# Cross-attention and sine feed-forward in one launch: the order of the first group

## The chip, the core and the metric

One core of a Trainium2 chip runs one program. The metric is the device time of a run in microseconds. The median of three runs of the kernel before is 244.93 us (244.87 to 245.15).

## The reference

The input x has 2 batches of 2048 rows of 512; the context has 2 batches of 77 keys of 512, with a mask of keys.

```
Q = layernorm(x) @ Wq + bq;  K = ctx @ Wk + bk;  V = ctx @ Wv + bv
scores = Q K^T / sqrt(512), masked keys at -1e9
x2 = x + softmax(scores) V @ Wo + bo
h = layernorm(x2)
out = x2 + sqrt((h @ cos(theta + theta_noise))^2 + (h @ sin(phi + phi_noise))^2)
```

## The kernel before

The rows go in 8 groups of 512, that is 4 tiles of 128 rows; groups alternate between the two batches. In a group n, TensorE multiplies the transposed h of each tile (`hT`, made by a DMA transpose from `h_split`) by the cosine matrix (real part, `re_bank`) and the sine matrix (imaginary part, `im_bank`). Values and weights are split into high and low fp16 halves, so each product is three matmuls per chunk of 128 (L503 to L505), 12 for a tile and part. Between them stand the attention matmuls of group n + 1 (`attend`) and the score matmuls of group n + 2.

All engines' queues are written out by hand, as lists of calls. Semaphores hold the order between engines; within an engine the order of the list is the order of execution. SP issues nearly all DMAs (loads, stores, transposes), and a wait in its list holds back all that stands behind it.

The change touches only what comes before the steady loop: the loads, the preparation of keys and values, and the first group. What is computed there:

* TensorE makes the keys and a folded query matrix (L428 to L450), then `scores(0, 0)`, the four chunks of V (`values_of(c)`, L525), and their product with Wo for each batch (`project_values(b, k)`, L533): batch 0 in `prep[0]`, batch 1 in `pT_bank`, the bank that also takes the transposed probabilities. Batch 0's bias is added by VectorE (L1108), batch 1's by a matmul (L541), and ScalarE copies batch 1's (L835).
* The first group's attention is done in fp32 by `attend_first(j)` (L468), from `probsT` and `vw[:, 0, :]`. Its first two matmuls wait for no residual, the others for the one two tiles back.
* V is then scaled and stacked in fp16 for all later groups: its norm goes through TensorE (L646), VectorE (L1126), POOL (L398 to L401), ScalarE (L844), VectorE (L1136) and three DMAs (L312, L317, L318). `attend(1, 1, 0)` waits for those and for the transposed probabilities of group 1 (`transpose_probs(1)`).
* The cosine and sine matrices are made in halves: the sum of theta and noise (`sum_theta`, VectorE), or of phi and noise (an accumulating DMA of POOL, `add_noise`), then `turns_of` (ScalarE), `reduce_angle` (VectorE), `sine` and `high_half_of_sine` (ScalarE), `low_half_of_sine` (VectorE).
* The first group's products go by halves of two chunks, `feed_first(j, part, half)` (L491), six matmuls each; `imag_and_score` puts scores of group 2 between them.
* `keep_busy(n)` (L464) issues n matmuls of zeros by zeros, 128x128 by 128x512 in fp16, into a bank that nobody reads.

Of the kernel before, what the change touches and what calls it, by code (L numbers as in the profile page):

```python
# [70 lines left out]
def build(nc, x, xT, ctxT, mask, Wk, WqT, Wv, Wo, bq, bk, bv, bo, theta, theta_noise, phi, phi_noise, out):  # L71
    with ExitStack() as ctx:
# [156 lines left out]
        def _(sp):  # L229
            def load_x(batch, blk):  # L230
                sp.dma_start(xb[batch][:, :, :], x[batch, blk]).then_inc(x_loaded[batch], 16)

            def load_xT(batch, blk):
                sp.dma_start(xTb[:, :, :], xT[batch, blk]).then_inc(xT_loaded, 16)

            def load_theta(c):
                cols_ = slice(DIM * c, DIM * c + DIM)
                sp.dma_start(angle_w[0][:, cols_], theta[:, cols_]).then_inc(ld_theta[c], 16)
                sp.dma_start(angle_n[0][:, cols_], theta_noise[:, cols_]).then_inc(ld_theta[c], 16)
# [5 lines left out]
            def load_second_x(j):  # L245
                sp.dma_start(xb[1][:, j, :], x[1, 0, :, j, :]).then_inc(ld_second_x[j], 16)
# [8 lines left out]
            load_x(0, 0)  # L255
            sp.dma_start(wv[:, :, :], Wv).then_inc(ld_wv, 16)
            sp.dma_start(wo[:, :, :], Wo).then_inc(ld_wo, 16)
            load_second_x(0)
            load_second_x(1)
            load_theta(0)  # L260
            load_theta(1)
            load_second_x(2)
            load_second_x(3)
            load_theta(2)
            load_theta(3)
# [5 lines left out]
            def transpose_h(m, tiles):  # L271


                for j in tiles:
                    sp.wait_ge(lo_made, TILES * m + j + 1)
                    sp.sem_inc(transposes_sent, 1)
                    sp.dma_start_transpose(hT[j][:, :, :, :].rearrange("p s c r -> p (s c) r"),
                                           h_split[j][:, :, :].rearrange("p s d -> p (s d)")).then_inc(hT_ready[j], 16)
# [29 lines left out]
            transpose_h(0, [2])  # L308
            sp.wait_ge(scores_mm, 2)
            load_xT(0, 1)  # L310
            sp.wait_ge(vw_hi_ready, 1)
            sp.dma_start(vw_stack[1][REST - KEYS:REST, :, :],  # L312
                         vw_stack[0][0:KEYS, :, :]).then_inc(vw_stacked, 16)
            sp.wait_ge(x2_made, TILES)
            load_x(0, 1)
# [23 lines left out]
        def _(pool):  # L339
# [18 lines left out]
            def rstd_of_x(m):  # L358

                pool.wait_ge(mean1_made, m + 1)  # L360
                nc.gpsimd.tensor_tensor(veps1[:, :], mv1[:, :, 1], eps[:, :], ALU.add).then_inc(eps1_added, 1)  # L361
                pool.wait_ge(eps1_added, m + 1)
                nc.gpsimd.tensor_tensor(rstd1[:, :], veps1[:, :], minus_half[:, :], ALU.pow).then_inc(rstd1_made, 1)
# [27 lines left out]
            rstd_of_x(1)  # L391
# [8 lines left out]
            nc.gpsimd.tensor_scalar(vw_scale[:, :], vw_norm_inv[:, :], V_SCALE, None, ALU.mult).then_inc(vw_scale_made, 1)  # L400
            nc.gpsimd.tensor_scalar(total_scale[:, :], vw_norm_inv[:, :], V_SCALE * P_SCALE, None,  # L401
# [15 lines left out]
        def _(pe):  # L417
# [46 lines left out]
            def keep_busy(n):  # L464
                for _ in range(n):
                    nc.tensor.matmul(re_bank[1][:, :], warm[:, 0:P], warm[:, :], start=True, stop=True)

            def attend_first(j):  # L468

                if j >= 2:  # L470
                    pe.wait_ge(x2_made, j - 1)
                nc.tensor.matmul(att_bank[j % 2][:, :], probsT[:, P * j:P * j + P], vw[:, 0, :],
                                 start=True, stop=True).then_inc(att_mm, 1)
# [17 lines left out]
            def feed_first(j, part, half):  # L491

                if half == 0 and part == 0:
                    pe.wait_ge(hT_ready[j], 16)
                elif half == 0:
                    pe.wait_ge(re_squared, j + 1)
                if j == 0:
                    pe.wait_ge(w_ready, 2 * part + half + 1)
                product(prep[j], j, part, range(CH // 2 * half, CH // 2 * half + CH // 2))
# [25 lines left out]
            def values_of(c):  # L525

                bank_ = prep[2 + c] if c < 2 else prep[4 + c]
                for k in range(CH):
                    last = nc.tensor.matmul(bank_[:, 0:KK], wv[:, k, P * c:P * c + P], ctx_t[:, k, :],
                                            start=(k == 0), stop=(k == CH - 1))  # L530
                last.then_inc(vT_mm, 1)

            def project_values(b, k):  # L533

                bank_ = pT_bank if b else prep[0]
                pe.wait_ge(vT_ready, k + 1)
                last = nc.tensor.matmul(bank_[0:KEYS, :], vT[:, k, KEYS * b:KEYS * b + KEYS], wo[:, k, :],
                                        start=(k == 0), stop=(k == CH - 1 and b == 0))
                if k == CH - 1:
                    if b == 1:  # L540
                        last = nc.tensor.matmul(bank_[0:KEYS, :], ones_keys[0:1, 0:KEYS], bo_rows[0:1, :],  # L541
                                                start=False, stop=True)
                    last.then_inc(vw_mm, 1)
# [73 lines left out]
            values_of(1)  # L617
            pe.wait_ge(ld_wo, 16)
            pe.wait_ge(c_ready, 1)
            project_values(0, 0)  # L620
            values_of(2)
            project_values(0, 1)
            values_of(3)
# [7 lines left out]
            keep_busy(4)  # L631
# [3 lines left out]
            pe.wait_ge(pT_copied, 1)  # L635
            project_values(1, 0)
# [7 lines left out]
            keep_busy(3)  # L644
            pe.wait_ge(key_norm_made, 1)
            nc.tensor.matmul(pT_bank[:, 0:1], ones_keys[:, :], key_norm[:, :], start=True, stop=True).then_inc(vw_norm_mm, 1)  # L646
            attend_first(3)
            feed_first(0, 0, 0)
            keep_busy(2)
            feed_first(0, 0, 1)  # L650
            feed_first(1, 0, 0)
            feed_first(1, 0, 1)
            feed_first(0, 1, 0)
            feed_first(2, 0, 0)
            feed_first(0, 1, 1)
            feed_first(2, 0, 1)
            imag_and_score(1, 0, 0)
            imag_and_score(1, 1, 4)
            pe.wait_ge(vw_stacked, 3 * 16)
# [25 lines left out]
        def _(act):  # L685
# [131 lines left out]
            values_turned(0)  # L817
            values_turned(1)
            exps(0)
            values_turned(2)  # L820
            act.wait_ge(quarter_made, 1)
            turns_of(0, 0)
            values_turned(3)
            nc.scalar.activation(act_scratch[:, 1:2], zero[:, :], ACT.Sin)
            act.wait_ge(pT_mm, 1)
            nc.scalar.activation(probsT[:, :], pT_bank[0:KEYS, :], ACT.Copy).then_inc(pT_copied, 1)
            sine(0, 0)
            turns_of(0, 1)
            high_half_of_sine(0, 0)
            sine(0, 1)  # L830
            high_first(0)
            high_half_of_sine(0, 1)
            turns_of(1, 0)
            act.wait_ge(vw_mm, 2)
            nc.scalar.activation(vw[:, 1, :], pT_bank[0:KEYS, :], ACT.Copy).then_inc(vw_ready, 1)  # L835
            high_first(1)
            act.wait_ge(vw_ready, 2)
            nc.scalar.activation(vw_squares[:, :, :], vw[:, :, :], ACT.Square, accum_out=key_norm[:, :]).then_inc(key_norm_made, 1)
            high_first(2)
            turns_of(1, 1)  # L840
            sine(1, 0)
# [5 lines left out]
            square_first(0, 0)  # L847
            high_half_of_sine(1, 1)
            exps(1)
            high_probs(1)  # L850
            square_first(1, 0)
            high_first(3)
            square_first(2, 0)
# [49 lines left out]
        def _(dve):  # L903
# [135 lines left out]
            def stats_and_mean(m, b, j):  # L1039

                stats_of_x2(m, b, j)
                dve.wait_ge(stats2_made, TILES * m + j + 1)
                mean_of_x2(m, j)
# [43 lines left out]
            stats_of_x(0, 0, [3])  # L1087
# [3 lines left out]
            nc.vector.tensor_tensor(c_keys[:, :], c_mid[:, :], keep_off[:, :], ALU.add).then_inc(c_ready, 1)  # L1091
            dve.wait_ge(stats1_made, 1)
            mean_of_x(0)
            logits_of(0, 0)
            stats_of_second_x(0)
            top_of(0)
            stats_of_second_x(1)
            sum_theta(0)
            sum_theta(1)
            stats_of_second_x(2)  # L1100
            stats_of_second_x(3)
            softmax_total(0)
            reduce_angle(0, 0)
            dve.wait_ge(stats1_made, 2)
            mean_of_x(1)
# [3 lines left out]
            sum_theta(2)  # L1109
            sum_theta(3)  # L1110
            residual(0, 0, 0)
            stats_and_mean(0, 0, 0)
            reduce_angle(0, 1)
            residual(0, 0, 1)
            normal_first(0)
            stats_and_mean(0, 0, 1)
            residual(0, 0, 2)
            low_half(0, 0)
            stats_and_mean(0, 0, 2)
            normal_first(1)  # L1120
            low_half_of_sine(0, 0)
            normal_first(2)
            low_half(0, 1)
            reduce_angle(1, 0)
            dve.wait_ge(vw_norm_mm, 1)
            nc.vector.tensor_scalar(vw_norm[:, :], pT_bank[:, 0:1], TINY, None, ALU.max).then_inc(vw_norm_read, 1)  # L1126
            low_half_of_sine(0, 1)
            low_half(0, 2)
            reduce_angle(1, 1)
            residual(0, 0, 3)  # L1130
            low_half_of_sine(1, 0)
            logits_of(1, 1)
            top_of(1)
            low_half_of_sine(1, 1)
# [4 lines left out]
            stats_and_mean(0, 0, 3)  # L1139
            low_probs(1)  # L1140
            dve.wait_ge(total_scale_made, 1)
            softmax_total(1)
            normal_first(3)
            low_half(0, 3)
            stats_of_x(0, 1, [0])
            stats_of_x(0, 1, [1])
            residual(1, 1, 0)
            stats_and_mean(1, 1, 0)
            stats_of_x(0, 1, [2])
            residual(1, 1, 1)  # L1150
            stats_of_x(0, 1, [3])
            stats_and_mean(1, 1, 1)
            low_half(1, 0)
            dve.wait_ge(stats1_made, 3)
            mean_of_x(2)
            residual(1, 1, 2)
            stats_and_mean(1, 1, 2)
            low_half(1, 1)
# [4 lines left out]
            add_squares_first(0)  # L1163
# [110 lines left out]
```

## Time and profile before

| | |
|---|---|
| median of 3 runs | 244.93 us |
| the profiled execution's own time | 245.31 us |
| its span | 243.2 us |
| TensorE busy | 235.8 us, 97% |
| VectorE busy | 169.6 us, 70% |
| ScalarE busy | 145.9 us, 60% |
| POOL busy | 54.4 us, 22% |
| DMA bytes moved | 44.80 MB |

The profile is of one execution. Times in it count from the start of the span. The time of a run is longer than the span by what lies around it, 2.1 us here. Busy time of TensorE counts matmuls that overlap in the pipeline once.

### The profile page before, as it was taken

How to read it: one execution, taken by the hardware profiler on the slowest of the kernel's cores; microseconds unless marked ns; L12 is line 12 of the kernel's file. 1: busy time of each engine (PE TensorE's matmuls, PEld its weight loads, DVE VectorE, ACT ScalarE, POOL GpSimd, SP SyncE). 2: the span in 40 equal slices, each digit the busy share in tenths (PEclk: the TensorE clock that was granted, in tenths of full speed). 3: DMA queues.
4: the chain of work that ended last, by engine and by line, in shares of the span. 5: the costliest groups of instructions: out<-in, count | busy, mean ns of one | idle time of the engine just before them, and what ended most of it. 6: DMA issues, size and time to landing. Idle time of an engine off the chain costs nothing.

```text
span 243.2 us, 3947 instructions
## 1 busy us (share of the span) xinstructions
PE 235.8 (97%) x1260; PEld 136.6 (56%) x1260; DVE 169.6 (70%) x341; ACT 145.9 (60%) x252; POOL 54.4 (22%) x154
## 2 busy tenths in 40 slices
PE   6999999999999999999999999999999999999993
PEld 2899437457544584458544854476447744444472
DVE  1676899976897876777768775877587753873443
ACT  2222787981669347943795379546873589266442
POOL 1002175410601233023302330132104310132000
PEclk9999999999999999999999999999999999999999
DMA  6999988695258724972397258734774324413622
GB/s 192 367 428 388 377 290 158 133 352 86 46 146 210 299 82 92 255 281 93 85 252 264 108 108 237 229 160 89 232 239 175 72 57 89 172 43 86 214 92 86
DMA packets 49533, 44.80 MB, mean 184 GB/s; under 512 B 42630, under 2 KB 42886, under 8 KB 46445
## 3 DMA queue, kind: packets, MB, share of 16 engines
q1 hardware_dynamic: 48565, 43.37, 57.7%
q0 software_dynamic: 288, 1.05, 2.4%
q10 hardware_dynamic: 664, 0.18, 0.3%
q8 instruction: 8, 0.13, 0.2%
q14 instruction: 8, 0.07, 0.1%
HBM read 25.66 MB, written 8.39 MB: 140 GB/s over the span
## 4 chain that ended last, share of the span: by engine, by line
PE 86%; DMA 7%; SPq 3%; ACT 2%; DVE 1%; issue 0%; DVEq 0%; ACTq 0%
PE re L503 9%; PE im L503 9%; PE im L504 9%; PE re L504 9%; PE re L505 9%; PE im L505 9%; PE score_bank L551 7%; DMA angle_n<-in_theta_noise 7%; PE att L481 3%; PE att L479 2%; PE re L564 2%; PE im L564 2%; PE re L566 2%; PE im L566 2%; PE re L568 2%; PE im L568 2%
## 5 line engine op out<-in xcount | busy, mean ns | idle before, releaser
L773 ACT ACTIVATE h<-x,shift,rstd 128x512 f32<-128x512 f32 x28 | 22.7, 811 | 34.6 <-POOL shift L382 34.6
L551 PEld LDWEIGHTS score_bank<-a_keys,xTb 128*128 128x128 f32 x192 | 35.9, 190 | 8.2
L503 PE MATMUL re<-w_hi,hT 128*128 128x512 f16 x100 | 37.9, 379 | 0.0
L503 PE MATMUL im<-w_hi,hT 128*128 128x512 f16 x100 | 37.9, 379 | 0.0
L505 PE MATMUL re<-w_hi,hT 128*128 128x512 f16 x100 | 37.9, 379 | 0.0
L505 PE MATMUL im<-w_hi,hT 128*128 128x512 f16 x100 | 37.9, 379 | 0.0
L504 PE MATMUL re<-w_lo,hT 128*128 128x512 f16 x100 | 37.9, 379 | 0.0
L504 PE MATMUL im<-w_lo,hT 128*128 128x512 f16 x100 | 37.9, 379 | 0.0
L1055 DVE SCALAR_TENSOR_TENSOR h_split<-h,h_split 128x512 f16<-128x512 f32 x32 | 22.1, 692 | 20.9 <-ACT h_split L777 20.2
L551 PE MATMUL score_bank<-a_keys,xTb 128*128 128x77 f32 x192 | 32.8, 252 | 0.0
L792 ACT ACTIVATE sq_re<-re 128x512 f32<-128x512 f32 x27 | 15.8, 586 | 17.2 <-PE re L505 12.1
L1024 DVE SCALAR_TENSOR_TENSOR x<-att,inv_total,xb 128x512 f32<-128x512 f32 x32 | 23.5, 735 | 2.9 <-PE att L481 2.9
L1077 DVE TENSOR_TENSOR wv<-x,wk 128x2048 f32<-128x2048 f32 x7 | 16.1, 2293 | 10.5 <-ACT wk L807 5.8
L1030 DVE BATCH_NORM_STATS2 stats<-x 128x6 f32<-128x512 f32 x32 | 22.2, 693 | 0.9
L375 POOL TENSOR_TENSOR veps<-mv,eps 128x1 f32<-128x1 f32 x28 | 6.1, 217 | 72.0 <-DVE mv L1037 72.0
L361 POOL TENSOR_TENSOR veps<-mv,eps 128x4 f32<-128x4 f32 x8 | 4.4, 550 | 79.4 <-DVE mv L972 79.4
L1069 DVE TENSOR_TENSOR wk<-sq_re,sq_im 128x512 f32<-128x512 f32 x27 | 18.5, 684 | 1.0 <-ACT sq_im L792 0.3
L958 DVE BATCH_NORM_STATS2 stats<-xb 128x6 f32<-128x512 f32 x28 | 17.4, 679 | 1.4 <-DMA xb<-in_x 1.4
L777 ACT ACTIVATE h_split<-h 128x512 f16<-128x512 f32 x28 | 17.6, 630 | 1.2
L792 ACT ACTIVATE sq_im<-im 128x512 f32<-128x512 f32 x27 | 15.9, 588 | 1.6 <-PE im L505 1.5
L503 PEld LDWEIGHTS re<-w_hi,hT 128*128 128x128 f16 x100 | 9.8, 98 | 12.4 <-DMA hT<-h_split 0.8
L504 PEld LDWEIGHTS re<-w_lo,hT 128*128 128x128 f16 x100 | 9.8, 98 | 11.9 <-issue 0.3
(181 smaller groups left out, 425.7 us busy)
## 6 DMA issues: line engine op xcount, KB each, us to landing
xTb<-in_xT SPq DMA_DIRECT2D x8, 1024.0 KB, 5.2
xb<-in_x SPq DMA_DIRECT2D x7, 1024.0 KB, 5.5
out_rows<-wv SPq DMA_DIRECT2D x7, 1024.0 KB, 3.9
wk<-in_Wk SPq DMA_DIRECT2D x2, 512.0 KB, 5.5
wqT<-in_WqT SPq DMA_DIRECT2D x4, 256.0 KB, 7.8
wv<-in_Wv SPq DMA_DIRECT2D x1, 1024.0 KB, 13.6
wo<-in_Wo SPq DMA_DIRECT2D x1, 1024.0 KB, 16.1
xb<-in_x SPq DMA_DIRECT2D x4, 256.0 KB, 16.2
```

The source lines that it names most:

```text
L503: nc.tensor.matmul(bank_[:, :], hT[j][:, 0, k, :], w_hi[part][:, k, :], start=(k == 0), stop=False)
L504: nc.tensor.matmul(bank_[:, :], hT[j][:, 0, k, :], w_lo[part][:, k, :], start=False, stop=False)
L505: last = nc.tensor.matmul(bank_[:, :], hT[j][:, 1, k, :], w_hi[part][:, k, :], start=False, stop=(k == CH - 1))
L551: last = nc.tensor.matmul(score_bank[:, KEYS * j:KEYS * j + KEYS], xTb[:, k, P * j:P * j + P], a_keys[:, k, KEYS * batch:KEYS * batch + KEYS],
L773: nc.scalar.activation(h[j % 2][:, :], x2[b][:, j, :], ACT.Identity, bias=shift2[:, j:j + 1], scale=rstd2[:, j:j + 1]).then_inc(h_made, 1)
L777: nc.scalar.activation(h_split[j][:, 0, :], h[j % 2][:, :], ACT.Copy, scale=H_SCALE).then_inc(hi_made, 1)
L792: nc.scalar.activation((sq_re, sq_im)[part][j % 2][:, :], (re_bank, im_bank)[part][j % 2][:, :], ACT.Square, scale=UNSCALE).then_inc((re_s ...
L958: last = nc.vector.bn_stats(stats1[:, j, :], xb[b][:, j, :])
L1024: nc.vector.scalar_tensor_tensor(out=x2[b][:, j, :], in0=att_bank[j % 2][:, :], scalar=inv_total[:, j:j + 1], in1=xb[b][:, j, :], op0=ALU. ...
L1030: nc.vector.bn_stats(stats2[:, j, :], x2[b][:, j, :]).then_inc(stats2_made, 1)
L1055: nc.vector.scalar_tensor_tensor(out=h_split[j][:, 1, :], in0=h[j % 2][:, :], scalar=H_SCALE, in1=h_split[j][:, 0, :], op0=ALU.mult, op1=A ...
L1069: nc.vector.tensor_tensor(power[:, j, :], sq_re[j % 2][:, :], sq_im[j % 2][:, :], ALU.add).then_inc(power_made, 1)
```

## The change

Every edit is one of order, except three: batch 1's product with Wo gets `prep[1]` (the bank `re_bank[1]`) in place of `pT_bank`, `keep_busy` writes to `im_bank[1]` in place of `re_bank[1]`, and of the zero matmuls, groups of four, three and two become groups of two and two.

* SP: theta's four quarters (each a load of theta and one of its noise) stand ahead of Wv, Wo and the second x. Later, the load of x transposed for group 2 goes ahead of the transpose of tile 2's h, and the load of x for group 2 ahead of the stacking of V.
* POOL: `rstd_of_x(1)` goes from the front to behind the scale of V.
* TensorE: all four `values_of` come ahead of the projections; `project_values(1, 0)` ahead of the first attention; `attend_first(3)` ahead of the norm of V; `feed_first(2, 0, 0)` ahead of `feed_first(0, 1, 0)`.
* ScalarE and VectorE: their lists are laid out anew, as the diff shows.

```diff
 SP
             load_xT(0, 0)
             load_x(0, 0)
+            load_theta(0)
             sp.dma_start(wv[:, :, :], Wv).then_inc(ld_wv, 16)
+            load_theta(1)
             sp.dma_start(wo[:, :, :], Wo).then_inc(ld_wo, 16)
+            load_theta(2)
+            load_theta(3)
             load_second_x(0)
             load_second_x(1)
-            load_theta(0)
-            load_theta(1)
             load_second_x(2)
             load_second_x(3)
-            load_theta(2)
-            load_theta(3)
             load_phi(0)
...
             transpose_h(0, [1])
-            transpose_h(0, [2])
             sp.wait_ge(scores_mm, 2)
             load_xT(0, 1)
+            transpose_h(0, [2])
+            sp.wait_ge(x2_made, TILES)
+            load_x(0, 1)
             sp.wait_ge(vw_hi_ready, 1)
...
-            sp.wait_ge(x2_made, TILES)
-            load_x(0, 1)
 POOL
             rstd_of_x(0)
-            rstd_of_x(1)
             add_noise(0)
...
             nc.gpsimd.tensor_scalar(vw_scale[:, :], ...)
+            rstd_of_x(1)
 TensorE
-                bank_ = pT_bank if b else prep[0]
+                bank_ = prep[b]
...
             values_of(0)
             values_of(1)
+            values_of(2)
+            values_of(3)
...
             project_values(0, 3)
-            keep_busy(4)
+            project_values(1, 0)
             pe.wait_ge(vw_ready, 1)
             pe.wait_ge(pT_copied, 1)
             attend_first(0)
-            pe.wait_ge(pT_copied, 1)
-            project_values(1, 0)
             attend_first(1)
...
             scores(1, 1)
-            keep_busy(3)
+            attend_first(3)
             pe.wait_ge(key_norm_made, 1)
             ... (the norm of V)
-            attend_first(3)
             feed_first(0, 0, 0)
             keep_busy(2)
             feed_first(0, 0, 1)
+            pe.wait_ge(vw_ready, 2)
             feed_first(1, 0, 0)
             feed_first(1, 0, 1)
+            feed_first(2, 0, 0)
             feed_first(0, 1, 0)
-            feed_first(2, 0, 0)
-            feed_first(0, 1, 1)
             feed_first(2, 0, 1)
             imag_and_score(1, 0, 0)
+            feed_first(0, 1, 1)
             imag_and_score(1, 1, 4)
+            keep_busy(2)
             pe.wait_ge(vw_stacked, 3 * 16)
             attend(1, 1, 0)
 ScalarE
             values_turned(0)
+            turns_of(0, 0)
             values_turned(1)
             exps(0)
             values_turned(2)
-            turns_of(0, 0)
             values_turned(3)
             ... (the load of the sine table)
+            turns_of(0, 1)
             ... (probsT <- pT_bank)
             sine(0, 0)
-            turns_of(0, 1)
+            sine(0, 1)
             high_half_of_sine(0, 0)
-            sine(0, 1)
+            high_half_of_sine(0, 1)
             high_first(0)
-            high_half_of_sine(0, 1)
+            ... (vw[:, 1, :] <- re_bank[1])
             turns_of(1, 0)
-            ... (vw[:, 1, :] <- pT_bank)
             high_first(1)
             ... (the squares of V)
+            sine(1, 0)
             high_first(2)
             turns_of(1, 1)
-            sine(1, 0)
             high_half_of_sine(1, 0)
             ... (vw_stack <- vw)
             sine(1, 1)
             square_first(0, 0)
+            square_first(1, 0)
             high_half_of_sine(1, 1)
             exps(1)
             high_probs(1)
-            square_first(1, 0)
+            square_first(2, 0)
             high_first(3)
-            square_first(2, 0)
 VectorE
             mean_of_x(0)
-            logits_of(0, 0)
-            stats_of_second_x(0)
-            top_of(0)
-            stats_of_second_x(1)
             sum_theta(0)
             sum_theta(1)
+            logits_of(0, 0)
+            top_of(0)
+            reduce_angle(0, 0)
+            sum_theta(2)
+            softmax_total(0)
+            sum_theta(3)
+            stats_of_second_x(0)
+            stats_of_second_x(1)
             stats_of_second_x(2)
-            stats_of_second_x(3)
-            softmax_total(0)
-            reduce_angle(0, 0)
-            dve.wait_ge(stats1_made, 2)
-            mean_of_x(1)
             ... (vw[:, 0, :] <- prep[0] + bo_rows)
-            sum_theta(2)
-            sum_theta(3)
+            reduce_angle(0, 1)
             residual(0, 0, 0)
             stats_and_mean(0, 0, 0)
-            reduce_angle(0, 1)
             residual(0, 0, 1)
-            normal_first(0)
             stats_and_mean(0, 0, 1)
             residual(0, 0, 2)
+            normal_first(0)
+            low_half_of_sine(0, 0)
             low_half(0, 0)
+            normal_first(1)
             stats_and_mean(0, 0, 2)
-            normal_first(1)
-            low_half_of_sine(0, 0)
+            reduce_angle(1, 0)
+            low_half(0, 1)
             normal_first(2)
-            low_half(0, 1)
-            reduce_angle(1, 0)
+            low_half_of_sine(0, 1)
             ... (vw_norm <- pT_bank)
-            low_half_of_sine(0, 1)
             low_half(0, 2)
+            stats_of_second_x(3)
             reduce_angle(1, 1)
+            dve.wait_ge(stats1_made, 2)
+            mean_of_x(1)
             residual(0, 0, 3)
             low_half_of_sine(1, 0)
             logits_of(1, 1)
+            stats_and_mean(0, 0, 3)
             top_of(1)
-            low_half_of_sine(1, 1)
             ... (vw_lo)
-            stats_and_mean(0, 0, 3)
+            low_half_of_sine(1, 1)
             low_probs(1)
```

The rest of VectorE's list up to the loop is moved by one to four places likewise: the statistics of x for group 2 stand ahead of the residuals of group 1, `add_squares_first(0)` ahead of `low_half(1, 1)`.

## Rows read from the trace of the kernel before

**Rows 1.** The page, busy time by engine and TensorE's clock in 40 slices.

```profile
PE 235.8 (97%) x1260; PEld 136.6 (56%) x1260; DVE 169.6 (70%) x341; ACT 145.9 (60%) x252; POOL 54.4 (22%) x154
...
PEclk9999999999999999999999999999999999999999
```

**Rows 2.** Windows: length, busy time of each engine, clock, DMA share, GB/s.

```profile
28.00:30.00 2.00, 1.88 (x6) 0.60 (x6) 2.00 (x7) 1.97 (x5) 0.58 (x1) 1.00 1.03 343
...
70.00:90.00 20.00, 20.00 (x111) 11.64 (x109) 15.44 (x30) 12.38 (x23) 4.45 (x14) 1.00 0.64 198
```

**Rows 3.** The page, the chain that ended last: shares of the span by engine.

```profile
PE 86%; DMA 7%; SPq 3%; ACT 2%; DVE 1%; issue 0%; DVEq 0%; ACTq 0%
```

**Rows 4.** Timeline of TensorE: start, length, line, what, count, idle time before it.

```profile
1.19 4.23 PE L422 MATMUL att<-warm 128*128 128x512 f16 x11 [1.19 <-DVE warm L905]
6.39 1.29 PE L428 MATMUL re<-ctx_t,wk 128*128 128x154 f32 x8 [0.97 <-DMA wk<-in_Wk]
...
20.33 2.31 PE L529 MATMUL im<-ctx_t,wv 128*128 128x154 f32 x16
...
29.04 1.03 PE L466 MATMUL re<-warm 128*128 128x512 f16 x4
30.21 1.10 PE L472 MATMUL att<-vw,probsT 77*128 77x512 f32 x2
...
41.04 0.81 PE L466 MATMUL re<-warm 128*128 128x512 f16 x3
...
43.05 0.38 PE L503 MATMUL re<-w_hi,hT 128*128 128x512 f16 x1
...
44.34 0.59 PE L466 MATMUL re<-warm 128*128 128x512 f16 x2
...
58.07 0.38 PE L479 MATMUL att<-vw_stack,pT 128*128 128x512 f16 x1
```

**Rows 5.** Timeline of the weight loads, first product of tile 1.

```profile
46.26 0.10 PEld L503 LDWEIGHTS re<-w_hi,hT 128*128 128x128 f16 x1 [0.53 <-DMA hT<-h_split]
```

**Rows 6.** Timeline of VectorE, 26 to 38 us.

```profile
26.49 1.33 DVE L965 BATCH_NORM_STATS2 stats<-xb 128x6 f32<-128x512 f32 x2
...
29.32 0.69 DVE L1108 TENSOR_TENSOR vw<-re,bo_rows 77x512 f32<-77x512 f32 x1
...
31.35 0.75 DVE L1024 SCALAR_TENSOR_TENSOR x<-att,inv_total,xb 128x512 f32<-128x512 f32 x1
...
36.81 0.68 DVE L1055 SCALAR_TENSOR_TENSOR h_split<-h,h_split 128x512 f16<-128x512 f32 x1
```

**Rows 7.** DMA issues at 5.42 (Wv), 5.92 (Wo) and 19.81: KB, us to landing.

```profile
wv<-in_Wv SPq DMA_DIRECT2D x1, 1024.0 KB, 13.6
wo<-in_Wo SPq DMA_DIRECT2D x1, 1024.0 KB, 16.1
...
angle_n<-in_theta_noise SPq DMA_DIRECT2D x1, 256.0 KB, 10.9
```

**Rows 8.** DMA issues at 37.59; at 69.44 and 70.04; at 77.81 and 76.40.

```profile
hT<-h_split SPq DMA_TRANSPOSE x1, 5.0
...
xb<-in_x SPq DMA_DIRECT2D x1, 1024.0 KB, 5.5
hT<-h_split SPq DMA_TRANSPOSE x1, 5.8
...
xTb<-in_xT SPq DMA_DIRECT2D x1, 1024.0 KB, 4.8
hT<-h_split SPq DMA_TRANSPOSE x1, 2.7
```

**Rows 9.** Timeline of ScalarE, the first turns of phi.

```profile
38.71 1.06 ACT L725 ACTIVATE turns<-angle_w 128x1024 int32<-128x1024 f32 x1 [1.67 <-DMA angle_w<-in_phi_noise]
```

**Rows 10.** DMA issues at 52.88 and at 74.46, transposed probabilities.

```profile
pT<-p_split SPq DMA_TRANSPOSE x1, 4.3
...
pT<-p_split SPq DMA_TRANSPOSE x1, 3.1
```

More of the change, by code:

```diff
@@ L465, in keep_busy @@
                 for _ in range(n):
-                    nc.tensor.matmul(re_bank[1][:, :], warm[:, 0:P], warm[:, :], start=True, stop=True)
+                    nc.tensor.matmul(im_bank[1][:, :], warm[:, 0:P], warm[:, :], start=True, stop=True)
             def attend_first(j):
@@ L620, in _ @@
             project_values(0, 0)
-            values_of(2)
             project_values(0, 1)
-            values_of(3)
             project_values(0, 2)
@@ L817, in _ @@
             values_turned(0)
+            act.wait_ge(quarter_made, 1)
+            turns_of(0, 0)
             values_turned(1)
@@ L820, in _ @@
             values_turned(2)
-            act.wait_ge(quarter_made, 1)
-            turns_of(0, 0)
             values_turned(3)
             nc.scalar.activation(act_scratch[:, 1:2], zero[:, :], ACT.Sin)
+            turns_of(0, 1)
             act.wait_ge(pT_mm, 1)
@@ L827, in _ @@
             sine(0, 0)
-            turns_of(0, 1)
+            sine(0, 1)
             high_half_of_sine(0, 0)
-            sine(0, 1)
+            high_half_of_sine(0, 1)
             high_first(0)
-            high_half_of_sine(0, 1)
+            act.wait_ge(vw_mm, 2)
+            nc.scalar.activation(vw[:, 1, :], re_bank[1][0:KEYS, :], ACT.Copy).then_inc(vw_ready, 1)
             turns_of(1, 0)
-            act.wait_ge(vw_mm, 2)
-            nc.scalar.activation(vw[:, 1, :], pT_bank[0:KEYS, :], ACT.Copy).then_inc(vw_ready, 1)
             high_first(1)
@@ L1086, in _ @@
             stats_of_x(0, 0, [2])
-            stats_of_x(0, 0, [3])
             dve.wait_ge(c_mm, 1)
@@ L1091, in _ @@
             nc.vector.tensor_tensor(c_keys[:, :], c_mid[:, :], keep_off[:, :], ALU.add).then_inc(c_ready, 1)
+            stats_of_x(0, 0, [3])
             dve.wait_ge(stats1_made, 1)
             mean_of_x(0)
-            logits_of(0, 0)
-            stats_of_second_x(0)
-            top_of(0)
-            stats_of_second_x(1)
             sum_theta(0)
             sum_theta(1)
-            stats_of_second_x(2)
-            stats_of_second_x(3)
-            softmax_total(0)
-            reduce_angle(0, 0)
-            dve.wait_ge(stats1_made, 2)
-            mean_of_x(1)
+            logits_of(0, 0)
[6 more added lines that the diff above has]
+            stats_of_second_x(1)
+            stats_of_second_x(2)
             dve.wait_ge(ld_bo, 16)
@@ L1138, in _ @@
                                            op1=ALU.subtract).then_inc(vw_lo_ready, 1)
-            stats_and_mean(0, 0, 3)
+            low_half_of_sine(1, 1)
             low_probs(1)
+            normal_first(3)
+            stats_of_x(0, 1, [0])
+            low_half(0, 3)
+            stats_of_x(0, 1, [1])
             dve.wait_ge(total_scale_made, 1)
             softmax_total(1)
[L1143 to L1146, printed above, removed]
+            stats_of_x(0, 1, [2])
+            stats_of_x(0, 1, [3])
             residual(1, 1, 0)
             stats_and_mean(1, 1, 0)
[L1149 to L1153, printed above, removed]
             dve.wait_ge(stats1_made, 3)
             mean_of_x(2)
+            residual(1, 1, 1)
+            stats_and_mean(1, 1, 1)
             residual(1, 1, 2)
+            low_half(1, 0)
             stats_and_mean(1, 1, 2)
+            add_squares_first(0)
             low_half(1, 1)
@@ L1162, in _ @@
             low_half(1, 2)
-            add_squares_first(0)
             add_squares_first(1)
```

## The prediction

> **What bounds the kernel now.** I read the page's busy shares first. TensorE is busy for 97% of the span and the page shows its clock at the upper level in all 40 slices [rows 1]. The table of busy time by stretch then says where the missing 3% is: TensorE is busy 1.88 of the 2 us from 28 to 30, and all of the 20 us from 70 to 90 [rows 2]. The chain of waits has 86% of the span on TensorE, 7% in a DMA and 2% on ScalarE [rows 3]; those two lie ahead of the first attention matmul, at 30.21. So the kernel is one queue of TensorE work that starts late: nothing later than the first group can give time back, and whatever the first group loses or gains moves the end by the same amount. I therefore follow one number, the start of the first attention matmul on the stacked values (`attend(1, 1, 0)`), at 58.07 us in the TensorE timeline [rows 4]. Before it TensorE already waits for transposed h tiles: the weight load of tile 1 stands until 46.26 [rows 5], and tile 0's h lands at 42.6, only 0.4 ahead of its first product at 43.05 [rows 4, 8].
>
> **What the change takes out.** Nine zero matmuls go (4, 3 and 2 by the timeline's groups), four come (two stay at their place, two new). The groups take 29.04 to 29.90, 41.04 to about 41.7, and 44.34 to 44.77 [rows 4], so one is worth 0.215 us. The diff keeps the two of 44.34, so seven go and two come, net five, or 1.08 us of TensorE time. That is a gain only where TensorE would not have waited in their place. The four of 29.04 stood in front of a wait: `attend_first(0)` starts at 30.21 because the addition that makes the first V (VectorE, 29.32 for 0.69) ends at 30.01 [rows 6]. In their place the change puts `project_values(1, 0)`, two passes of 0.43 us, possible because it now has a bank of its own.
>
> **The loads.** SP puts theta(0) ahead of Wv, theta(1) ahead of Wo, and theta(2), theta(3) ahead of the four second-x tiles. The bytes in all are the same, so I move each load to the time at which as many bytes had landed before. Wv is issued at 5.42 and lands 13.6 later, 19.0; Wo at 5.92 plus 16.1, 22.0; the last theta noise at 19.81 plus 10.9, 30.7 [rows 7]. From Wo to there are 12 pieces of 256 KB in 8.7 us, 0.73 each. Wv moves by two pieces to 20.4: the scores before it end at 20.33 [rows 4], so TensorE loses 0.1. Wo moves by four pieces to about 24.7: TensorE now has all four `values_of` first (the timeline shows 16 instructions, two calls, in 2.14 us), until 20.4 + 4.2 = 24.6, so again 0.1. The last theta noise comes to the place of the last second-x tile, which VectorE's statistics show landed by 27.1 [rows 6], and the third second-x tile to the place between that and 30.7, about 29.4 (28.6 to 30.0).
>
> **The start of the attention.** TensorE: Wo at 24.7, three projections (2.6), transposes (0.5), the fourth (0.86) and `project_values(1, 0)` (0.86) give 29.6. VectorE now has the statistics of three second-x tiles ahead of the addition: the third starts at its landing, 29.4, takes 0.6, the addition 0.7, and TensorE starts 0.2 after that, as now: 30.9 (30.6 to 31.3). ScalarE is not late: turns of the second theta half 27.9 to 28.95, then the copy of the probabilities to 29.5. So the first attention moves from 30.21 to 30.9, with 0.86 of work already done: 0.2 gained, and 0.65 more from the three zero matmuls of 41.04. From the first attention to the end of the scores it is 10.8 us now (30.21 to 41.04), 10.0 without one projection, so 40.9; `attend_first(3)` and the norm's matmul take 1.1: TensorE reaches `feed_first(0, 0, 0)` at 41.9 to 42.0, against 43.05 now.
>
> **What is late next.** hT of tile 0. The first residual is at 31.35 now, 1.14 after the attention, so 32.04. By the spacings of VectorE's rows: residual 0.78, statistics and mean 0.83 (twice each), third residual 0.66, normal 0.47, low half of the sine 1.15, low half of h 0.64: 38.2, against 36.81 + 0.68 = 37.5 now [rows 6]. The transpose of 37.59 takes 5.0, until 42.6, while the phi noise is in flight [rows 8]; issued 0.7 later, into the same DMA work, I let it land between 42.7 and 43.3. So the 1.1 us that TensorE gained stand as a wait, and the first product starts at about 43.0, as now. Tile 1's low half stays at 41.6, because ScalarE's turns of phi wait for the phi noise (38.71 for 1.06 [rows 9]), and its transpose lands at about 46.2 as now: `feed_first(1, 0, 0)` at 46.35, against 46.27. All that lies before it is worth nothing.
>
> **The reordered transposes.** `load_xT(0, 1)`, 1 MB, is issued now at 45.80, after the transpose of tile 2; the change puts it ahead of it, at about 42.95, right after that of tile 1; scores(1, 1), its condition, has ended at 40.9. hT of tile 2 is issued at 43.95 and is needed earlier than before, since `feed_first(2, 0, 0)` moves one half product (1.295) forward: 46.35 + 2 x 1.295 = 48.95. The one pair of this kind in the trace: x load at 69.44 (5.5) and a transpose at 70.04, which takes 5.8 instead of 2.7, so it lands 0.9 after the load [rows 8]. An xT load lands 4.8 after its issue [rows 8], which gives 42.95 + 4.8 + 0.9 = 48.65, and by the x load 49.35. I take 49.1 and 0.1 to start: 49.2, a wait of 0.25. From there to the attention on stacked values: four half products (5.18), two halves of imaginary and scores (2.0 each), 0.43 of zero matmuls, 9.6: 58.85, against 58.07. That is +0.8.
>
> The Trainium skill ("DMA: Bandwidth & Descriptors", queues, rings and completion order) says that each DMA engine takes a queue's descriptors in ring order; the 5.8 us of the trace agrees. Its section on the anatomy of one DMA fits 2.0 us plus bytes over 436 GB/s, by which (an estimate) load and transpose together would be down at about 48.0 and nothing waits; that is the first rival's place.
>
> **The rest of the first group.** The probabilities are later: `square_first(1, 0)` is now ahead of the high half of the last sine on ScalarE and waits for TensorE until 49.2; the half ends at 50.65, table load (1.28), four exponentials and the split end at 54.1 to 54.5, against 52.2, and the low half at 54.6 to 55.0. The pT transpose is issued 52.88 now and takes 4.3 beside an x load; that load is now issued near 46.7, so I use the undisturbed 3.1 [rows 10]: 57.8 to 58.2, before 58.85. With 4.3 it would be 58.9 to 59.3. On POOL `rstd_of_x(1)` goes behind the scale of V (45.2) and ends by 49.0, its reader, the logits, at 49.8 before `imag_and_score(1, 0, 0)` at 53; the low half of the last sine is done at 53.4, before 55.1. The vw stack needs 52.2 + 2 to 3. Later edits in order only move VectorE work inside cover of 1 us or more.
>
> **Sum.** 0.1 (tile 1) + 0.25 (tile 2) + 0.43 (two new zero matmuls) = +0.8 us against the profiled execution, 245.31 us (span 243.2 and 2.1 around it): 246.1. The median shown, 244.93, is 0.4 lower, so 245.7. A run's spread is some 0.3 us; from 0.2% (0.49 us) on a difference can be told.
>
> **Rivals.** (a) Tile 2 isn't late: a transpose takes 2.7, and 1 MB at the 1 MB in 2.4 us of the best stretches is out of its way by 48.0. Only 0.1 and the two matmuls stay, +0.5: 245.4. For it: 4.8 for xT; against it: 5.8. Chance 0.23. (b) Transposes land early: tile 0 and 1 in 2.7 each (41.0, 44.4), since less collides with them; TensorE starts at 41.9, reaches tile 2 at 47.6 and the attention at 57.2 to 57.7 with pT then last: -0.4 to -0.9, 244.3. For it: the 2.7 of the undisturbed ones; against it: phi noise is in flight until 41.7 in both. Chance 0.2. (c) pT last: 4.3 us from 55.0, +1.3: 246.2. Chance 0.07. (d) The clock. The zero matmuls filled idle time; now TensorE idles 1.2 us at 29.6 and 1.1 at 41.9. The first eleven matmuls stand 0.43 us apart (4.23 us for all) and 0.215 later, which is 1.2 against 2.4 GHz. A fall that lasts as long as those eleven costs half of 4.2, of which 1 us may hide in the wait at 42: +1.1 on top of the sum, 246.8 by the median; it decides from the first f16 product that starts 0.43 after its forerunner. Against it: the trace holds the upper level after 0.97 us of idle at 6.39 [rows 4]. Chance 0.07. (e) The forecast, 0.43.
>
> The Trainium skill ("TensorE: Matmul & The Clock Gate", HAM oscillation) has the clock fall when TensorE idles between groups of matmuls; this trace shows no fall.
>
> **Numbers.** Faster by over 0.49: most of (b) and a little of (e), 0.2. Within: part of (a) and (e), 0.25. Slower: the rest, 0.55. The range: 244.2 takes in most of (b), 246.9 takes in (c) and (d) in its lighter form.
>
> **What would show it.** The weight load of `feed_first(2, 0, 0)` waiting for hT until 49.1 (right), or no wait there (rival a). TensorE idle at about 29.6 to 30.9 for the first V, and 41.9 to 43.0 for hT of tile 0. `attend(1, 1, 0)` at 58.85; 57.5 says (b), a wait for pT there says (c), spacing of 0.43 in f16 products after either idle stretch says (d). The prediction is wrong if hT of tile 1 lands a microsecond earlier than 46.2, or if the second-x tiles land after 30.5 and push V out past 32.

## The result and the profile after

The changed kernel is slower: 247.33 us median of 5 runs (246.41 to 247.74), the kernel before beside it 245.15. The ratio is 1.0071, 95% interval 1.0036 to 1.0106: 1.7 us, where 0.8 was forecast. Taken on the 244.93 of the front, 1.0071 is 246.7, inside the range; the raw median lies above it. The profiled execution took 247.33 us, its span is 245.4, so 2.2 us more than before. The ratios, here and in the experiments, leave out executions that took over 1.5% more than the fastest of their kernel.

The page after, to be read beside [rows 1, 3]:

```profile
PE 235.0 (96%) x1255; PEld 136.1 (55%) x1255; DVE 169.3 (69%) x341; ACT 146.2 (60%) x252; POOL 55.6 (23%) x154
...
PE 78%; SPq 9%; DMA 8%; DVE 2%; POOL 1%; issue 1%; ACT 0%; DVEq 0%
```

TensorE does 0.8 us less work, and the span grew by 2.2: 3 us more are waits. SP's queue and the DMAs now have 17% of the chain, against 10% before. The table of stretches (columns as in [rows 2]) says where:

```profile
28.00:30.00 2.00, 1.85 (x6) 0.42 (x4) 2.00 (x5) 1.75 (x3) 0.00 (x0) 1.00 1.09 436
30.00:32.00 2.00, 1.29 (x3) 0.68 (x4) 1.91 (x4) 1.09 (x2) 0.47 (x1) 1.00 0.99 416
...
48.00:50.00 2.00, 0.52 (x3) 0.02 (x1) 1.97 (x8) 2.00 (x4) 0.36 (x2) 1.00 1.16 323
50.00:52.00 2.00, 1.41 (x7) 0.70 (x8) 2.00 (x3) 1.97 (x5) 1.92 (x2) 1.00 1.00 398
...
70.00:90.00 20.00, 20.00 (x105) 10.81 (x103) 15.66 (x31) 13.08 (x24) 3.72 (x11) 1.00 0.70 211
```

TensorE's timeline after, against [rows 4]:

```profile
20.53 2.37 PE L529 MATMUL im<-ctx_t,wv 128*128 128x154 f32 x16
...
30.71 1.98 PE L472 MATMUL att<-vw,probsT 77*128 77x512 f32 x4 [0.86 <-DVE vw L1106]
...
42.23 0.39 PE L503 MATMUL re<-w_hi,hT 128*128 128x512 f16 x1 [0.34 <-DMA hT<-h_split]
43.54 0.59 PE L466 MATMUL im<-warm 128*128 128x512 f16 x2
45.77 0.38 PE L503 MATMUL re<-w_hi,hT 128*128 128x512 f16 x1 [0.34 <-DMA hT<-h_split]
50.59 0.39 PE L503 MATMUL im<-w_hi,hT 128*128 128x512 f16 x1 [2.07 <-DMA hT<-h_split]
59.80 0.59 PE L466 MATMUL im<-warm 128*128 128x512 f16 x2
60.23 0.38 PE L479 MATMUL att<-vw_stack,pT 128*128 128x512 f16 x1
```

The first matmul on the stacked values moved from 58.07 to 60.23, +2.16, and that is the whole loss. The row at 50.59 is `feed_first(2, 0, 0)`: TensorE is idle for 2.07 us until tile 2's transposed h is there. SP's timeline, and then the us from issue to landing of the DMAs issued at 41.64, 43.78 and 44.47, say why:

```profile
38.11 1.52 SPq L277 DMA_TRANSPOSE hT<-h_split  x1
41.64 2.09 SPq L277 DMA_TRANSPOSE hT<-h_split  x1
43.78 0.58 SPq L234 DMA_DIRECT2D xTb<-in_xT  x1
44.47 1.23 SPq L277 DMA_TRANSPOSE hT<-h_split  x1
```

```profile
hT<-h_split SPq DMA_TRANSPOSE x1, 4.0
...
xTb<-in_xT SPq DMA_DIRECT2D x1, 1024.0 KB, 5.7
...
hT<-h_split SPq DMA_TRANSPOSE x1, 6.1
```

The load lands at 49.5 and the transpose behind it at 50.6, 1.1 later. In the kernel before, where the load came behind it, this transpose (issued at 44.52) took 2.8 us:

```profile
hT<-h_split SPq DMA_TRANSPOSE x1, 2.8
```

### The profile page after: what moved, and what is told of

The parts are those of the page before. It is cut to its first block, busy times and chain, and to the rows that moved or that the text cites. A ratio compares the mean times of both kernels' runs of the same rounds, so it can differ in the third digit from the quotient of the medians.

```text
span 245.4 us, 3937 instructions
## 1 busy us (share of the span) xinstructions
PE 235.0 (96%) x1255; PEld 136.1 (55%) x1255; DVE 169.3 (69%) x341; ACT 146.2 (60%) x252; POOL 55.6 (23%) x154
## 4 chain that ended last, share of the span: by engine, by line
PE 78%; SPq 9%; DMA 8%; DVE 2%; POOL 1%; issue 1%; ACT 0%; DVEq 0%
PE im L503 9%; PE im L504 9%; PE im L505 9%; PE re L503 8%; PE re L505 8%; PE re L504 8%; PE score_bank L551 7%; DMA angle_w<-in_phi 5%; PE att L481 2%; DMA hT<-h_split 2%; PE att L479 2%; SPq L238 2%; PE re L564 2%; PE im L564 2%; PE im L568 2%; PE re L566 2%
## 5 line engine op out<-in xcount | busy, mean ns | idle before, releaser
L361 POOL TENSOR_TENSOR veps<-mv,eps 128x4 f32<-128x4 f32 x8 | 3.7, 464 | 71.8 <-DVE mv L971 71.8
L503 PEld LDWEIGHTS im<-w_hi,hT 128*128 128x128 f16 x100 | 9.8, 98 | 14.1 <-DMA hT<-h_split 2.6
```

Source lines behind the costliest of these rows:

```text
L503: nc.tensor.matmul(bank_[:, :], hT[j][:, 0, k, :], w_hi[part][:, k, :], start=(k == 0), stop=False)
```

## The experiments

### Tile 2's transpose ahead of the load (e1)

```diff
             transpose_h(0, [1])
+            transpose_h(0, [2])
             sp.wait_ge(scores_mm, 2)
             load_xT(0, 1)
-            transpose_h(0, [2])
```

> The changed kernel with one edit: SP issues the transpose of tile 2's h ahead of the load of x transposed for group 2, as before the change. Theory A (the 1 MB load ahead of it in SP's queue makes the transpose late): issued at about 43.8, it lands by 46.6 to 47.8, TensorE starts feed_first(2, 0, 0) at about 48.35 without a wait, and attend(1, 1, 0) stands at 58.1 to 58.6 instead of 60.23: 1.6 to 2.1 us faster than the changed kernel, so 0.998 to 1.002 of the kernel before. Theory B (transposes in this stretch are slow by themselves, for the phi noise and the longer issues): it takes 4 to 6 us here too, lands at 48 to 50, and at least 1 us of the 2.07 us wait stays: ratio 1.003 or more.

Ratio to the kernel before 0.9983 (0.9965 to 1.0001). Tile 2's transpose, issued at 44.70, and TensorE at the attention on stacked values:

```profile
hT<-h_split SPq DMA_TRANSPOSE x1, 2.7
```

```profile
57.53 0.59 PE L466 MATMUL im<-warm 128*128 128x512 f16 x2
57.96 0.38 PE L479 MATMUL att<-vw_stack,pT 128*128 128x512 f16 x1
```

It lands at 47.4, no wait for tile 2 is left, and 60.23 became 57.96. One line of SP's list was the whole loss: theory A. B asked for 4 to 6 us here and is out.

### The same line in the kernel before (e2)

```diff
             transpose_h(0, [1])
-            transpose_h(0, [2])
             sp.wait_ge(scores_mm, 2)
             load_xT(0, 1)
+            transpose_h(0, [2])
```

> The kernel before with one edit: SP issues the load of x transposed for group 2 ahead of the transpose of tile 2's h, as the change does. Theory A: the transpose takes about 6 us as in the changed kernel and lands at 50 to 50.6, but here its first reader starts at 51.46, so TensorE waits for nothing new and the ratio is 0.999 to 1.001. Theory C (the early load itself costs, by whatever it collides with, not by this one wait): slower by 1 us or more even here, 1.004 or more. Theory B: the transpose takes under 4 us.

The reader's time in that text is mistaken: 51.46 is where a later half starts, tile 2's first product stands at 50.16 in the kernel before. The transpose took 5.6 us and landed at 50.2, so there is a small wait. The kernel before, then this run:

```profile
50.16 0.38 PE L503 MATMUL im<-w_hi,hT 128*128 128x512 f16 x1
```

```profile
hT<-h_split SPq DMA_TRANSPOSE x1, 5.6
...
50.27 0.39 PE L503 MATMUL im<-w_hi,hT 128*128 128x512 f16 x1 [0.34 <-DMA hT<-h_split]
...
58.18 0.38 PE L479 MATMUL att<-vw_stack,pT 128*128 128x512 f16 x1
```

Ratio 1.0034 (1.0013 to 1.0055), some 0.8 us: more than theory A's 1.001, and theory C's 1.004 lies inside the interval. The profiled execution, at 245.32, was the fastest of its kernel and shows only 0.11 us (58.18 against 58.07). Whether the others waited longer at the same place, or the early load also costs elsewhere in this kernel (theory C), is not shown. In the changed kernel nothing is left for C: the one wait and e1 account for the loss.

### Tile 2's product in its old place (e3)

```diff
             feed_first(1, 0, 1)
-            feed_first(2, 0, 0)
             feed_first(0, 1, 0)
+            feed_first(2, 0, 0)
```

> The changed kernel with one edit: TensorE does feed_first(0, 1, 0) ahead of feed_first(2, 0, 0), as before the change. Theory A: the transpose still lands at 50.5, but its reader comes at 49.65 instead of 48.35, so the wait is 2.07 - 1.30 = 0.8 us, attend(1, 1, 0) at about 58.9, ratio about 1.002 to 1.005 (1.3 us faster than the changed kernel). Theory D (the new place of feed_first(0, 1, 0) is what matters, its sine half would be late): a new wait for the low half of the sine, ready at 48.1, appears, and nothing is gained.

```profile
49.07 0.39 PE L503 MATMUL re<-w_hi,hT 128*128 128x512 f16 x1 [0.33 <-ACT wk L781]
50.80 0.39 PE L503 MATMUL im<-w_hi,hT 128*128 128x512 f16 x1 [0.26 <-DMA hT<-h_split]
```

Ratio 1.0024 (1.0005 to 1.0043), the attention at 59.14, 1.1 us earlier. The transpose takes 6.1 us as in the changed kernel and lands at 50.8, the waits fall from 2.07 to 0.33 and 0.26. The first is neither theory's: `feed_first(0, 1, 0)` waits for the square of tile 0's real part.

### Without the two zero matmuls ahead of the stacked attention (e4)

```diff
 (e1, and)
             imag_and_score(1, 1, 4)
-            keep_busy(2)
             pe.wait_ge(vw_stacked, 3 * 16)
```

> As e1_tile2_first, and the two zero matmuls ahead of attend(1, 1, 0) taken out. If TensorE is the bound there: another 0.43 us, attend(1, 1, 0) at 57.7. If the transposed probabilities are last (issued at 54.35, 3.1 to 4.3 us): TensorE waits for them until 57.5 to 58.6, and the zero matmuls only filled that wait: 0 to 0.4 us. Ratio to the kernel before 0.996 to 1.001. Clock theory: if the zero matmuls keep the upper clock, f16 products after the wait stand 0.43 apart instead of 0.215.

Ratio 0.9962 (0.9942 to 0.9983): with e1's line, this is faster than the kernel before. The attention on stacked values starts at 57.19:

```profile
57.19 0.38 PE L479 MATMUL att<-vw_stack,pT 128*128 128x512 f16 x1
```

That is 0.8 earlier than in e1, but the whole first group began 0.6 earlier in this execution. From the first attention it is 26.80 us, against 26.98 in e1, so 0.18 is what the trace gives to the two: tile 1 was waited for 0.27 us here and not there. The clock stayed up, 1.00 over the span.

### V's bank alone (e5)

```diff
-                bank_ = pT_bank if b else prep[0]
+                bank_ = prep[b]
...
             project_values(0, 3)
-            keep_busy(4)
+            project_values(1, 0)
```

> The kernel before with one part of the change: batch 1's V in the bank re_bank[1], so that project_values(1, 0) stands in place of the four zero matmuls ahead of the first attention; all orders else as before. Theory A (0.86 us of TensorE work is moved into a wait, and the time comes back as a wait for the transposed h of tile 0 and tile 1, which VectorE and the phi noise set): attention still starts at 30.2, TensorE reaches feed_first(0, 0, 0) at 42.2, waits for tile 0 until 42.6 and for tile 1 until 46.2 as now: 0 to 0.3 us gained, ratio 0.998 to 1.001. Theory E (zero matmuls on TensorE's queue are the cost): the full 0.86 us is gained, ratio 0.9965.

```profile
40.69 0.81 PE L466 MATMUL im<-warm 128*128 128x512 f16 x3
41.95 0.38 PE L644 MATMUL pT_bank<-key_norm,ones_keys 77*128 77x1 f32 x2 [0.45 <-ACT vw_squares L837]
...
43.14 0.38 PE L503 MATMUL re<-w_hi,hT 128*128 128x512 f16 x1
```

Ratio 1.0000 (0.9983 to 1.0016): theory E's 0.9965 is out, theory A's 0.998 to 1.001 holds. The trace alone would not do. In this execution TensorE reached the values of V 1.2 us late (21.57 against 20.33), and the first attention stood at 30.70 and not at 30.2, without a wait. By the first product that is made up, 43.14 against 43.05, and tile 1's product stands at 46.21 (46.27 before), with its transpose down at 46.07. One wait more than A named is there, the norm's for ScalarE's squares (0.45).

### The loads alone (e8)

```diff
+            load_theta(0)
             (Wv)
+            load_theta(1)
             (Wo)
+            load_theta(2)
+            load_theta(3)
             load_second_x(0)
 ... (theta's four calls behind it go)
```

> The kernel before with one part of the change: SP loads theta ahead of Wv, Wo and the second x, and nothing else. If the load order and the lists of the engines only fit together: the second project_values stands for Wo until 24.7, VectorE's statistics of the second x stand ahead of top_of(0) until 27.9, so the exponentials and the first attention are 2.5 to 3 us late: 33 instead of 30.2, ratio 1.008 to 1.013. If the load order matters little by itself: 0.999 to 1.002.

```profile
27.81 0.69 DVE L965 BATCH_NORM_STATS2 stats<-xb 128x6 f32<-128x512 f32 x1 [5.97 <-DMA xb<-in_x]
```

```profile
24.56 1.08 PE L537 MATMUL re<-wo,vT 128*77 128x512 f32 x2 [2.03 <-DMA wo<-in_Wo]
...
34.33 1.10 PE L472 MATMUL att<-vw,probsT 77*128 77x512 f32 x2
```

Ratio 1.0177 (1.0143 to 1.0211), beyond the expected 1.013. Both named waits are there, the one for Wo at the first projection and not at the second; the attention starts at 34.33, 1.3 later than forecast. Part of that is the clock, which fell after the 2.03 us of idle (granted clock 0.91, 0.50 and 0.74 in the three stretches):

```profile
24.00:26.00 2.00, 1.44 (x5) 0.92 (x6) 0.00 (x0) 0.00 (x0) 0.00 (x0) 0.91 1.05 391
26.00:28.00 2.00, 2.00 (x8) 1.62 (x7) 0.19 (x1) 0.00 (x0) 0.00 (x0) 0.50 1.06 409
28.00:30.00 2.00, 2.00 (x10) 1.26 (x8) 2.00 (x5) 1.09 (x7) 0.00 (x0) 0.74 1.06 426
```

So the load order needs the lists: alone it is a loss of 4 us. The lists without the load order were not run.

### Tiles 0 and 1 earlier (e6)

```diff
 (e4, and on VectorE)
+            normal_first(0)
             residual(0, 0, 2)
-            normal_first(0)
-            low_half_of_sine(0, 0)
             low_half(0, 0)
+            low_half_of_sine(0, 0)
...
+            low_half(0, 1)
             reduce_angle(1, 0)
-            low_half(0, 1)
...
-            low_half_of_sine(0, 1)
             ... (vw_norm <- pT_bank)
+            low_half_of_sine(0, 1)
 ScalarE
+            high_half_of_sine(1, 1)
             square_first(1, 0)
-            high_half_of_sine(1, 1)
```

> e4_tile2_first_no_zero with VectorE's list mended: low_half(0, 0) ahead of the low half of the first sine and normal_first(0) ahead of the third residual, low_half(0, 1) ahead of reduce_angle(1, 0), the read of V's norm ahead of low_half_of_sine(0, 1); on ScalarE the high half of the last sine ahead of square_first(1, 0). If the transposed h of tiles 0 and 1 is what TensorE waits for (as theory A has it): transposes issued at about 36.6 and 40.1 instead of 37.8 and 41.2, first product 0.3 us earlier, feed_first(1, 0, 0) at about 44.7 instead of 45.36, attend(1, 1, 0) at 56.4 to 56.6: 0.6 to 0.8 us under e4, ratio to the kernel before 0.992 to 0.995. If not (transposes land when the phi noise has, whatever their issue): same as e4, 0.996.

The attention on stacked values stands at 56.43, as expected, and the profiled execution took 243.63 us. The ratio, 0.9978 (0.9951 to 1.0005), is worse than the expected 0.992 to 0.995 and cannot be told from e4's. Of twelve executions three took 246.9 to 248.4 with a mean granted clock of 0.986 to 0.993, the others 243.6 to 245.2 at 0.996 to 1.000. The edit need not be the cause: of 24 executions of the kernel before beside it, four took 248.8 to 249.3 at 0.992 or 0.993.

Tile 0's transpose was issued 1.0 us earlier than in e4 (36.79 against 37.79) and landed only 0.3 earlier (41.59 against 41.89). The second phi noise was issued at 34.92 in both; e10 follows that up.

### V earlier, no zero matmuls (e7)

```diff
 (e6, and)
             stats_of_second_x(0)
-            stats_of_second_x(1)
-            stats_of_second_x(2)
             ... (vw[:, 0, :] <- prep[0] + bo_rows)
...
             feed_first(0, 0, 0)
-            keep_busy(2)
             feed_first(0, 0, 1)
 POOL
+            rstd_first(1)
             add_noise(1)
-            rstd_first(1)
```

> e6_tiles_early, with the statistics of second-x tiles 1 and 2 behind the addition that makes V instead of ahead of it, rstd_first(1) ahead of add_noise(1) on POOL, low_half_of_sine(0, 1) ahead of normal_first(2), and no zero matmul left but the eleven at the start. If the three statistics ahead of V are what holds the first attention: it starts at 29.6 to 29.8 instead of 30.4, TensorE reaches feed_first(0, 0, 0) at 40.8, and attend(1, 1, 0) stands at 55.6 to 56.5, with the transpose of tile 2 as the last wait: ratio 0.989 to 0.994. If the clock needs the zero matmuls: f16 products 0.43 us apart after a wait, and a ratio above e6's.

V came earlier (first attention at 29.92), and TensorE then waited the longer for tile 0. Its transpose was issued at 36.27, 0.5 earlier than in e6, and landed at 42.17, 0.6 later; the noise, now behind `rstd_first(1)`, was itself issued 0.5 later (35.41):

```profile
42.19 0.43 PE L503 MATMUL re<-w_hi,hT 128*128 128x512 f16 x1 [1.12 <-DMA hT<-h_split]
42.42 0.63 PE L504 MATMUL re<-w_lo,hT 128*128 128x512 f16 x1
42.84 0.63 PE L505 MATMUL re<-w_hi,hT 128*128 128x512 f16 x1
```

```profile
40.00:42.00 2.00, 1.07 (x5) 0.50 (x4) 2.00 (x3) 1.12 (x2) 1.31 (x1) 1.00 1.16 211
42.00:46.00 4.00, 3.81 (x10) 1.39 (x11) 3.97 (x12) 3.48 (x5) 1.27 (x3) 0.57 0.45 96
```

The granted clock is 0.57 of full from 42 to 46, that is mostly the lower level of 1.2 GHz, after a wait of 1.12 us. Of eight executions three took 243.8 to 244.1 at a mean clock of 0.999, the other five 245.4 to 248.6 at 0.982 to 0.993; that is more often than the four of 24 of the kernel before. The ratio, 0.9939 (0.992 to 0.9958), leaves three of the five out and hides this; the median of all eight is 246.15, that of the kernel before 245.39.

### The wait filled again (e9)

```diff
 (e6, and)
             project_values(1, 0)
+            keep_busy(3)
             pe.wait_ge(vw_ready, 1)
```

> e6_tiles_early with three zero matmuls (0.65 us) in the wait for V, between project_values(1, 0) and attend_first(0), where TensorE idles 0.86 us. If the idle stretches let TensorE's clock fall in some executions (e7's trace shows f16 products 0.43 us apart from 42.2 to 45.8 us, after 1.12 us of idle): the same 56.4 us for attend(1, 1, 0), and fewer executions at 247 us or more; ratio to the kernel before 0.992 to 0.996. If the fall has nothing to do with this wait: the same spread as e6, 0.998. If zero matmuls cost: 0.65 us more.

All seven executions lie between 243.88 and 244.57, at a mean clock of 0.996 or more; ratio 0.9959 (0.9942 to 0.9976), the attention at 56.60. So the three zero matmuls cost no more than the 0.17 us between 56.43 and 56.60, and not the 0.65 of the third theory. That they hold the clock up is not shown: none of the eleven executions of the kernel before beside them had a low clock either.

### The second phi noise later (e10)

```diff
 (e6, and on POOL)
-            add_noise(1)
             rstd_first(1)
             rstd_first(2)
+            add_noise(1)
```

> e6_tiles_early with POOL's second phi noise (add_noise(1)) behind rstd_first(2), so that it is issued at about 41.5 instead of 34.9. In the runs so far the transposed h of tile 0 landed 6.7 to 7.0 us after that DMA's issue, whether it was itself issued at 36.3 or at 38.4. If POOL's accumulating DMA holds it: it now lands 2.7 to 3.6 us after its own issue of 36.8, at 39.5 to 40.4, and that of tile 1, issued at 40.1, by 44.0. If transposes are slow there for another reason: 41.6 and 44.6 as in e6. The kernel as a whole gets slower (ScalarE's turns of the second phi half wait until 47 to 48): 246 to 249 us.

POOL's issue of the noise, then us to landing: both transposes issued at 37.00 and 39.98 (the median), the second of them alone, the noise, and the transpose issued at 43.91:

```profile
41.40 0.89 POOL L356 DMA_DIRECT2D angle_w<-in_phi_noise  x1
```

```profile
hT<-h_split SPq DMA_TRANSPOSE x2, 2.8
...
hT<-h_split SPq DMA_TRANSPOSE x1, 2.7
angle_w<-in_phi_noise POOLq DMA_DIRECT2D x1, 512.0 KB, 7.8
...
hT<-h_split SPq DMA_TRANSPOSE x1, 6.1
```

Tiles 0 and 1 take 2.8 and 2.7 us instead of 4.8 and 4.5, and tile 2, now beside the noise and with no load ahead of it, takes 6.1 and is waited for 2.59 us. The noise moved, and the slow transposes moved with it. The one execution took 249.69 us.

## Why the prediction was right in kind and short in size

* Loads: right. `values_of` starts at 20.53 (20.4 forecast), the fourth theta sum at 27.52, three second-x statistics end at 30.1, and the first attention starts at 30.71 (30.9).
* Tile 0: right in mechanism. The chain gave an issue at 38.2 (38.11), the product started at 42.23 against 43.0, because phi's loads and with them the second noise were 0.75 us earlier than before (35.22 against 35.98), which I had left as they were; in every trace tile 0 lands 6.6 to 7.1 us after that noise is issued (e10's, where it is moved away, apart).
* Tile 1: 45.77 against 46.35. It was issued as forecast, at 41.64, and took 4.0 us instead of 4.6. Why stays open: it took 4.0 in e2 too, with the noise as late as before (36.07).
* Tile 2: the step that was mis-sized. The wait was put at 0.25 us and measured 2.07 (2.23 from where the product would have started, 48.36, to 50.59). Its reader came 0.6 us earlier than forecast (48.36 against 48.95), and the transpose landed 1.5 later (50.6 against 49.1). Two terms made it late. The load was issued at 43.78 and not 42.95, as SP took 2.09 us over tile 1's transpose instead of the 1.23 assumed. And the load took 5.7 us, more than either row I had gone by (4.8 and 5.5), so that the transpose behind it took 6.1 from issue to landing where 5.15 was taken; that it lands 0.9 to 1.1 after the load was right. What made SP's issue long stays open: it is 2.08 in e3 and 2.01 in e4, 1.75 in e1, and 1.23 in e2 and e6.
* The two zero matmuls: 0.43 forecast, and 0.43 us is what the timeline shows (59.80 to 60.23); e4 gave 0.2 to 0.5 back.
* Probabilities (rival c) and early transposes (rival b): neither. pT was issued at 54.35 and took 3.1, as taken. Tiles 0 and 1 landed at 42.2 and 45.6, not at the 41.0 and 44.4 of (b). Rival (a) needed tile 2 down by 48.0, 2.6 us before it was. The fixed cost plus bytes of the Trainium skill ("DMA: Bandwidth & Descriptors", anatomy of one DMA), by which the estimate of 48.0 was made, is fitted there to DMAs that POOL issues; these two were SP's. Its ring order ("queues, rings and completion order") agrees with the 2.7 us of e1 against the 6.1 of the change.
* The clock (rival d) did not fall in the changed kernel's first group (1.00 in every stretch shown), but it did in the traces of e7, e8 and e10, so the rival was real. Its length fits e7 (1.2 GHz for nearly 4 us), its price of 1.1 us was low: e7's five executions with a low clock took 1.2 to 4.8 us more than its other three. And the clock line of [rows 1] proves less than the prediction made of it: in the kernel before, the profile prints 1.00 from 2 to 4 us, where the first matmuls stand 0.43 us apart.

Two lines of the change turn its sign. Of the 1.08 us of zero matmuls that it saves, 0.1 arrives in e1's trace (57.96 against 58.07), and its ratio cannot be told from 1. With e4's line as well the kernel is 0.9 us faster than before (0.9962), and with e6's order of tiles and a filled wait 1.0 (0.9959, attention at 56.60).

## What to carry to other kernels

Where one queue issues loads and transposes, look at the reader of each: a 1 MB load ahead of a transpose costs that transpose 3.4 us in the changed kernel (6.1 against 2.7) and 2.8 in the kernel before (5.6 against 2.8), and whether it costs the kernel anything depends on how early its reader stands (0.34 us of wait in e2, 2.07 after the change). A shortcut ahead of a wait (e5) gives nothing if the next wait is for a chain that did not start earlier. Where an engine's filler is cut, look at the clock of many runs and not of one profile, and at the same number of the kernel before beside them: e6's three executions with a low clock look like a finding only until its four are seen.

## What the runs showed of the hardware

* An accumulating DMA from POOL holds back transposes from SP. In eleven traces tile 0's landed 6.6 to 7.1 us after the issue of the second phi noise, whether issued itself at 36.3 (e7) or at 38.4 (e1), and 0.9 to 1.1 us after the noise had landed; with the noise out of the way 2.8 us after its own issue (e10). Tile 1's was slow too (3.7 to 4.9 us), even issued after the noise had landed (e5: 42.07 against 41.71, 4.0 us), and 2.7 with the noise moved (e10); how the one acts on the other is not shown.
* A transpose behind a 1 MB load on SP's queue lands 0.9 to 1.1 us after the load (before, [rows 8]; the change, e2, e3).
* TensorE's clock fell to 1.2 GHz after waits of 1.12 us (e7), 2.03 us (e8) and 2.59 us (e10: 0.50 from 50 to 52), and did not after 2.07 us in the changed kernel's trace. The Trainium skill's account ("TensorE: Matmul & The Clock Gate", HAM oscillation), that idle between groups lets it fall, agrees. That the mean clock is low in some executions of one kernel and not in others is in the times of e6, e7 and the kernel before; where in the execution it fell is seen in the profiled ones alone.
